# Last attention of a four-layer kernel: probabilities split into two 16-bit parts and turned by DMA instead of by TensorE

## What is computed

```python
N_HEAD = 32; D_MODEL = 512; N_KV_GROUPS = 8
D_HEAD = D_MODEL // N_HEAD            # 16
query = q @ w_q.T; key = k @ w_k.T; value = v @ w_v.T      # q = norm(x), k = v = context
scores = jnp.einsum('bghnd,bgsd->bghns', query, key) / D_HEAD ** 0.5
scores = jnp.where(mask, scores, jnp.finfo(scores.dtype).min)
attention = jax.nn.softmax(scores, axis=-1)
out = jnp.einsum('bghns,bgsd->bghnd', attention, value)
out = out.transpose(0, 3, 1, 2, 4).reshape(b, n, D_MODEL)
return out @ w_out.T
```

## Time and profile before

| | us |
|---|---|
| median of 3 runs | 1899.39 (1898.87 to 1901.48) |
| the profiled execution | 1895.06 |
| its span, first to last instruction | 1893.3 |
| L3's tiles, start of the first exp to start of the last | 232.1 (1497.57 to 1729.71) |
| mean granted TensorE clock (share of full speed) | 0.974 |

### The profile page before, as it was taken

One profiled execution on the slowest core, in us unless ns is written; L12 is line 12 of the kernel. 1 busy time (PEld: TensorE's weight loads), 2 busy tenths in 40 slices (PEclk: granted clock), 3 DMA queues, 4 the chain that ended last, 5 costly groups with the idle time before them and its releaser, 6 DMA issues.

```text
span 1893.3 us, 28955 instructions
## 1 busy us (share of the span) xinstructions
PE 1755.8 (93%) x9892; PEld 1421.6 (75%) x9892; DVE 1428.1 (75%) x3036; ACT 1048.9 (55%) x1999; POOL 882.5 (47%) x863
## 2 busy tenths in 40 slices
PE   6899999999897999989899999999989999998988
PEld 4677777777676887767688888888867788776755
DVE  6777887878767887766678777778764587786898
ACT  5766667666225565631556556556641387775333
POOL 6766776664633232044344444343346531232762
PEclk9999999999999999999999999999998999998998
DMA  5656656555517988762578778879762100120110
GB/s 185 145 101 144 134 115 142 117 125 112 131 25 142 209 189 174 140 134 73 110 152 196 149 170 173 172 156 194 150 142 101 53 1 23 46 91 29 67 45 23
DMA packets 524177, 226.13 MB, mean 119 GB/s; under 512 B 493696, under 2 KB 503168, under 8 KB 516736
## 3 DMA queue, kind: packets, MB, share of 16 engines
q1 hardware_dynamic: 524032, 224.28, 53.9%
HBM read 97.08 MB, written 5.24 MB: 54 GB/s over the span
## 4 chain that ended last, share of the span: by engine, by line
PE 68%; DVE 16%; DMA 4%; POOL 3%; ACT 3%; issue 3%; SPq 2%; DVEq 0%; POOLq 0%; ACTq 0%
PE ps_t L339 9%; PE ps_t L340 8%; PE ps_t L341 8%; PE ps_s L339 8%; PE ps_s L340 7%; PE ps_s L341 7%; PE ps_o L339 4%; PE ps_o L340 3%; PE ps_o L341 3%; PE ps_o L1887 3%; PE ps_t L1918 3%; PE ps_s L1873 2%; ACT ps_s L1250 2%; DVE nmax L1280 2%; DVE ps_s L1277 1%
## 5 line engine op out<-in xcount | busy, mean ns | idle before, releaser
L1250 ACT ACTIVATE ps_s<-ps_s,nmax 128x768 f32<-128x768 f32 (+1 forms) x320 | 252.6, 789 | 345.9 <-DVE nmax L1280 243.1
L1223 ACT ACTIVATE l_ab<-ps_s,rinv 128x768 f16<-128x768 f32 (+1 forms) x320 | 260.5, 814 | 69.0 <-DVE rinv L1325 54.1
L1318 DVE SCALAR_TENSOR_TENSOR l_ab<-ps_s,rinv,l_ab 128x768 f16<-128x768 f32 (+1 forms) x320 | 289.0, 903 | 2.5 <-ACT l_ab L1223 1.9
L1280 DVE TENSOR_REDUCE nmax<-ps_s 128x1 f32<-128x768 f32 x192 | 183.5, 956 | 124.9 <-PE ps_s L341 124.4
L339 PE MATMUL ps_o<-l_pt,l_v 128*128 128x256 f16 (+1 forms) x832 | 232.8, 280 | 20.2 <-DMA l_v<-l_vab 8.6
L340 PE MATMUL ps_o<-l_pt,l_v 128*128 128x256 f16 (+1 forms) x832 | 231.5, 278 | 0.0
L341 PE MATMUL ps_o<-l_pt,l_v 128*128 128x256 f16 (+1 forms) x832 | 231.5, 278 | 0.0
L339 PE MATMUL ps_s<-l_k_hi,l_q_hi 128*128 128x512 f32 (+3 forms) x512 | 186.3, 364 | 25.1 <-DVE l_ab L1318 21.4
L377 POOL TENSOR_TENSOR wo_hi<-raw_big,one 128x512 fp32r<-128x512 f32 (+2 forms) x100 | 102.5, 1025 | 209.7 <-PE ps_t L341 127.1
L340 PE MATMUL ps_s<-l_k_lo,l_q_hi 128*128 128x512 f32 (+3 forms) x512 | 179.6, 351 | 0.0
L341 PE MATMUL ps_s<-l_k_hi,l_q_lo 128*128 128x512 f32 (+3 forms) x512 | 179.0, 350 | 0.0
(11 more groups left out here) (386 smaller groups left out, 4955.3 us busy)
## 6 DMA issues: line engine op xcount, KB each, us to landing
raw_big<-in_l_wq SPq DMA_DIRECT2D x18, 1024.0 KB, 5.6
raw_big<-in_l_wo SPq DMA_DIRECT2D x18, 1024.0 KB, 5.8
w_raw<-in_f_w SPq DMA_DIRECT2D x32, 256.0 KB, 3.5
raw_big<-in_f_w SPq DMA_DIRECT2D x7, 1024.0 KB, 4.8
raw_kv<-in_l_wkv SPq DMA_DIRECT2D x12, 512.0 KB, 6.5
l_pt<-l_ab SPq DMA_TRANSPOSE x320, 3.7
raw_f<-in_f_w SPq DMA_DIRECT2D x4, 1024.0 KB, 4.8
w_nat<-in_f_w1n SPq DMA_DIRECT2D x16, 256.0 KB, 3.9
```

Of the source, the lines that this page charges most:

```text
L1223: e.activation(sp.ab[:, (k - 1) % 3, 0, :], self.scores_out(k - 1), ACT.Copy, scale=rinv[:, i:i + 1]).then_inc(s_pa, 1)
L1250: e.activation(self.scores_out(k), self.scores_out(k), ACT.Exp, bias=nmax[:, i:i + 1], scale=-1.0 if l.rope else 1.0, accum_out=rsum[:, i: ...
L1280: e.tensor_reduce(nmax[:, i:i + 1], o, AX.X, ALU.max, negate=True).then_inc(s_max, 1)
L1318: e.scalar_tensor_tensor(out=b, in0=self.scores_out(t), scalar=rinv[:, i:i + 1], in1=a, op0=ALU.mult, op1=ALU.subtract).then_inc(s_pb, 1)
```

## The change

- **Score banks**: five instead of four (`l3_bank`: the ring and `ps_t[0]`). DVE's `largest` now writes the masked scores back to the PSUM bank, and ACT's exp reads them there and writes `l3p` (four SBUF buffers) in float32. `scores` waits for exp, no longer for the maximum.
- **First part**: straight behind each exp, ACT writes `l3ab[k % 4][:, 0]` = float16(2^15 x p). It waits for its own exp and, from tile 4, for the DMA that turned tile k-4 (`wait_parts_free`).
- **Second part**: DVE, two slots later, `scalar_tensor_tensor` of `l3p` and the first part, both in SBUF, gives `l3ab[...][:, 1]` in float16.
- **Turn**: SP issues one DMA transpose a tile (128 x 1024 float16) into `l3pt` (five units); it waits for the second part and, from unit 5, for `attend` of unit u-5. PE's four transposes, ACT's copy and DVE's subtraction of them are gone.
- **attend** reads float16 operands, at slots k % 4 = 1 and 2 with a distance of 9 (before: k % 4 = 2 and 3, distance 6). The values are float16 too, scaled by a per-batch maximum, which needs a reduction, a diagonal and one matmul with ones for each of the two "v" jobs (slots -8 to -4, and 3 to 7), a scale on the two copies of `l3v`, and a scale in `l_o`.
- **Loads**: those of L3 and the first of the last feed-forward layer now stand in SP's loop between transposes (k = 10, 40, 72, 88, 102).
- The tail has three more slots (`slots3` ends at 138).

```diff
+            for k in range(1, N3 + 1):
+                i = k - 1
+                u = l3_unit(i)
+                e.wait_ge(s3["second_part"], i + 1)
+                if u >= 5:
+                    e.wait_ge(s3["pv"], u - 4)
+                e.dma_start_transpose(l3pt[u % 5][:, l3_tile(i)[3], :, :], l3ab[i % 4][:, :, :].rearrange("p a n -> p (a n)"))\
+                    .then_inc(s3_crossed[i % 4], 16)
+                if k == 10:
+                    load(e, "q", c3.q + 1, A["l3_wq"][1], ("o", c3.o + 1))
+                if k == 40:
+                    load(e, "o", c3.o + 1, A["l3_wo"][1], ("q", c3.q + 2))
+                if k in F3_LOADS_AT:
+                    f3_sp_ahead(e, F3_LOADS_AT.index(k))
...
             def scores(quad, qt):
...
-                if quad:
-                    e.wait_ge(s3["max"], 4 * quad - 2 + 2 * qt)
+                pair = 2 * quad + qt
+                if pair >= 2:
+                    e.wait_ge(s3["exp"], 2 * pair - 3)
...
-                if k % 4 >= 2 and 0 <= k - 6 < N3:
-                    attend((k - 6) // 4 * 2 + k % 2)
+                if k % 4 in (1, 2) and 0 <= k - 9 < N3:
+                    attend((k - 9) // 4 * 2 + (k - 1) % 4)
...
-                if 0 <= k - 2 < N3:
-                    i = k - 2
-                    o = take_turn_bank(piece_at3["t", i])
-                    e.wait_ge(s3["exp"], i + 1)
-                    for kk in range(4):
-                        mm = e.transpose(o[:, kk * P:(kk + 1) * P], l3p[:, i % 6, kk * P:(kk + 1) * P], ident[:, :])
...
-                    e.activation(l3p[:, k % 6, :], l3p[:, k % 6, :], ACT.Exp, bias=nmax[:, c:c + 1], scale=-1.0,
+                    if k >= 4:
+                        e.wait_ge(s3["second_part"], k - 3)
+                    e.activation(l3p[k % 4][:, :], l3_bank(k), ACT.Exp, bias=nmax[:, c:c + 1], scale=-1.0,
                                  accum_out=rsum[:, c:c + 1]).then_inc(s3["exp"], 1)
+                    wait_parts_free(e, k)
+                    e.wait_ge(s3["exp"], k + 1)
+                    e.activation(l3ab[k % 4][:, 0, :], l3p[k % 4][:, :], ACT.Copy, scale=P_SCALE).then_inc(s3["first_part"], 1)
...
+                if 0 <= k - 2 < N3:
+                    i = k - 2
+                    a, b = (l3ab[i % 4][:, part, :] for part in (0, 1))
+                    e.wait_ge(s3["first_part"], i + 1)
+                    e.scalar_tensor_tensor(out=b, in0=l3p[i % 4][:, :], scalar=P_SCALE, in1=a, op0=ALU.mult, op1=ALU.subtract)\
+                        .then_inc(s3["second_part"], 1)
```

More of the change, by code:

```diff
@@ L1661, in program @@
         c3 = START["l3"]
[L1662 removed]
+        s3 = {n: sem(f"l3_{n}") for n in ("S", "max", "exp", "first_part", "second_part", "rec", "aside", "aside_free", "vhi",
+                                         "vdiag", "vscale", "pv", "spread", "scaled", "ohi", "olo", "zero", "sel",
                                          "job_full", "job_hi", "job_out")}
+        s3_crossed = [sem(f"l3_probs_crossed_{i}") for i in range(4)]
         N3 = 4 * 32
@@ L1818, in l3_project @@
                 e.wait_ge(s3["job_out"], {4: 0, 5: 1, L3_JOBS - 1: j.n - 1}.get(j.n, j.n) or 1)
+            if part == 0 and j.n == L3_JOBS - 1:
+                e.wait_ge(s3["exp"], N3)
             o = j.bank()
```

210 lines of the change are left out of this document (112 added, 98 removed).

## The result

| | before | changed |
|---|---|---|
| median, us | 1899.13 (1896.24 to 1901.48) | 1908.16 (1905.54 to 1913.04) |
| ratio, with its 95% interval | | 1.0064 (1.0044 to 1.0085) |
| span of the profiled execution | 1893.3 | 1905.9 |
| L3, first exp to last exp | 232.1 | 237.5 |
| mean granted clock | 0.974 | 0.954 |

The forecast was 1890 us, range 1865 to 1912. The time lies inside the range, but on the other side of the kernel before. The ratio on record is not the quotient of these two medians of four runs each; that is 1.0048 and lies inside the interval too.

The account below looks back on a forecast made before the run. PE was taken to bound L3, 74.1 us of it transposes. Tiles 210, loads 9 and 1.5 more gave 220.5 us instead of 232.1; with head and tail 9.6 less, 1899.4 - 9.6 = 1890 us, range 1865 to 1912.

Parts of the forecast that it names:

- The pace of ACT and DVE: L3's tiles: ACT about 1.54 us and DVE 1.64 a tile; 103 tiles at 1.57, 24 at 2.0, 210 us.
- POOL in DVE's way: L3: POOL operations hold DVE's second parts, 12 us for 24 large ones and 6 for small ones, 18 together.
- The loads: 8 MB between L3's transposes make following ones late: 9 us in all, bounds 0 to 25.
- The sum: L3, first to last exp: 210 + 9 + 1.5 = 220.5 us instead of 232.1.
- a slack of 1.8 us a stop: L3: lateness of a transpose behind a load that costs nothing, set against 1.6, 4 and 6.7 us late.
- the upper bound, 25 us: L3's loads: 8 x 3.1 = 25 us if all of their time is paid.
- PE is no longer the bound: L3: without its transposes PE has 1.13 us of work a tile, no longer the bound unless its clock falls.
- The half clock: Rival, L3: PE at 1.2 GHz for part of its time makes the kernel slower, 1913 us; chance 0.18.
- f above 0.62 decides: Half-clock rival, L3: PE sets the pace if it runs at 1.2 GHz for over 0.62 of its time.
- DMA as the pace: Rival, L3: transposes and loads take the DMA engines 1.82 us a tile, no change, 1900 us; chance 0.15.
- Head and tail: L3's ends: head +1.5 us (0 to 3) for the reduction of v, tail +0.5 (0 to 2).
- the chance of "within": Whole kernel: chance of a result within about 0.2%, 3.8 us, of the kernel before, given as 0.15.

Follow-up runs that it names:

- e15: Changed kernel with loads in 256 KB pieces, second part a slot sooner, projections spread, weight splits of one column: ratio 0.9973 to before, L3 217.2 us.
- e8: The changed kernel run again without edits: ratio 1.0078 to the kernel before, L3 236.7 us.
- e1: Changed kernel with 5 of the 8 MB of loads moved behind L3's last transpose: ratio 1.0048 to the kernel before, L3 225.9 us.
- the square above: Changed kernel 1.0078 to before; projections and splits spread 1.0061; loads in pieces and second part sooner 1.0057; all of these 0.9998.
- e12: Changed kernel with loads in 256 KB pieces, second part a slot sooner, projections spread over other slots: ratio 1.0004 to before, L3 223.9 us.
- e10: Changed kernel with loads in pieces, second part sooner, half of each turn, projections without third product: ratio 1.0019 to before, L3 222.1 us.
- e3: Changed kernel with four extra PE matmuls ahead of each pair of scores: ratio 1.0097 to the kernel before, L3 241.5 us.
- e11: Changed kernel with loads in pieces, second part sooner, half of each turn, four more matmuls in each attend: ratio 1.0018 to before, L3 226.2 us.
- e9: Changed kernel with loads in 256 KB pieces, second part a slot sooner, only half of each turn: ratio 1.0045 to before, L3 226.0 us.
- e17: Changed kernel with second part sooner, projections spread, 3 MB of loads in pieces, 5 MB behind the last transpose: ratio 1.0014 to before, L3 226.4 us.

## Why the prediction was wrong, point by point

**The pace of ACT and DVE** held. I had 1.57 us a tile; undisturbed stretches run at 1.49 to 1.56. ACT's part is 1.39 (I had 1.43 and odd jobs). DVE's second part, in the group over L3's tiles:

```profile
L2047 DVE SCALAR_TENSOR_TENSOR l_ab<-l_p,l_ab x128: 678/689/1664, 1503.9 to 1741.4; 128x512 f16<-128x512 f32 x128
```

0.689 in the median, against the 0.744 I took from the earlier trace rows.

**POOL in DVE's way** was the right mechanism, too large. DVE and POOL of the changed kernel at one place:

```profile
1558.75 1.03 POOL L384 TENSOR_TENSOR wq_hi<-raw_big,one 128x512 fp32r<-128x512 f32 x1
1559.87 1.59 POOL L386 TENSOR_TENSOR wq_lo<-raw_big,wq_hi 128x512 fp32r<-128x512 f32 x1
```

```profile
1558.83 1.50 DVE L2047 SCALAR_TENSOR_TENSOR l_ab<-l_p,l_ab 128x512 f16<-128x512 f32 x1
```

The second part starts inside L384, ends 0.55 us behind its end, and takes 1.50 us, as in the earlier trace rows. The Trainium skill's rule on the page "SBUF — State Buffer" (section "SBUF: two separate sides") is what this row shows, and it holds the other way round as well: the POOL operation behind took 1.59 us instead of 1.29. I had 12 us for the 24 large operations; e15 gives 5 to 7 for them and for what they delay.

**The loads** are the first step that failed. The sum had 9 us, from a slack of 1.8 us a stop. The exps at the five loads came 25.2 us late (24.4 in e8), and ACT waited 29.3 us for transposes: nearly no slack hid anything. Taking 5 of the 8 MB away gave 11.5 us back in e1's trace and 3 to 6 by the ratios; the square above shows why, as other stops take a load stop's place. I had expected ACT to wait only behind the loads at k = 72 and 88, and it waited at all five. The slack was worked out at 1.57 us a slot. In the stretches between stops a slot is 1.39, so there is nearly none: second part done 1.4 us into slot k-2 plus 3.3 us of landing is 4.7, and ACT is there after 2 x 1.39 + 1.6 = 4.4. The 1.5 us until DVE wants the part, which I had counted too, are worth nothing where ACT itself sets the pace. That ACT alone is faster than the mean took away what was to hide the loads. I had named the upper bound, 25 us, and took the low side.

**"PE is no longer the bound"** is the second. The 1.13 us a tile are a mean, and a mean of 69% says nothing on a burst. PE is away for 3.0 to 5.5 us in each projection of 512 columns, and ACT has a stock of two or three tiles of 1.39 us. e12 puts this at 6 to 10 us, e10 at 4 to 6 for a third of it. The kernel before had the same projections; that with PE as the bound they cost their work and no more is argued, and no run takes them out of it.

**The half clock** came true, as a condition and not as the price that I had put on it: 0.80 in L3 instead of 0.98. I had "f above 0.62 decides" and f is about 0.4, and by mean work PE stays under the pace. It lengthens the bursts, and that has a price: 4.2 us in the first eight tiles between two executions of the same kernel, at 1.00 and at 0.68. So the rival had the right cause and the wrong path, the mean instead of the longest piece. PE work to keep the clock up cost more than it gave in e3; in e11 it gave nothing in the trace and 4.9 us by the medians. The rule of the Trainium skill (page "TensorE: Matmul & The Clock Gate", section "Part 4: PE-mode transpose") had made me halve this rival. The traces speak against that use of it: the rest of PE's work nearly all stayed, the stretch is as long, and the clock fell from 0.98 to 0.80 when they went. They don't settle it, since attend reads float16 now and PE's idle time lies in longer pieces.

**The order of DMA as the pace** (no change): in e9 half of the transposes' bytes are worth 2 to 4 us once the loads are in pieces, and e17 with a share of 0.89 is no shorter than e12 with 0.99. So the engines are close to the pace, but not it.

**Head and tail** were 1.5 and 0.5 us in the sum and measured 3.4 and 2.3, both outside my bounds (0 to 3 and 0 to 2). The first scores wait for 1.55 us of mask, then the reduction, the copy of v and the diagonal on DVE.

The account of L3: forecast 220.5, measured 237.5. Counted by place in the changed kernel's trace, the five loads are 25.2 us against 9 in the sum, which is the whole miss of the stage. All else is 212.3 us against 211.5, and that it fits is luck: I had 1.57 us a tile and 10 us for the splits, and it is 1.5 us a tile and 21.8 us of other stops, the long projections at half clock and POOL among them. These two are 9 less and 10 more. How the 21.8 divide was not taken apart, and the square above shows that no single edit can do it.

Two slips in the working change nothing: a single MB that is 1.6 us late against 1.8 us of slack costs nothing by that rule, where I wrote 0.5, and the chance of "within" adds up to 0.14, where I wrote 0.15.

By their stretches, e1 and e9 should equal the kernel before within 2 us, and their ratios say 9 us slower. Their profiled executions are 4.9 and 6.3 us under their medians, which is more than half of it; the rest is open.

## What to carry to other kernels

When the busiest engine is relieved, do not sum the others' means: walk the longest piece of its work that can't be interrupted, and count the tiles in stock on the other side. A queue on which nobody waited may hold any load; once results pass through it, every byte in it has its price, and slack must be worked out at the fastest pace of the stage, not at its mean. 74 us taken from the busiest engine brought nothing: its work had been the thing behind which 8 MB of loads, the projections and the splits stood hidden. And where two kinds of stop hide each other, test them together before calling either cheap: here each alone was 0.2% and both 0.8%.
